# One core, attention-like pooling: the goods of a pair fetched in two transfers instead of four, and TensorE's wait for pooled banks moved to the head of a round

## The reference

```python
outer = jnp.einsum('bi,bnj->bnij', candidate_ad, goods).reshape(Bs, Ns, Ks * Ks)
k_b = jnp.broadcast_to(candidate_ad[:, None, :], (Bs, Ns, Ks))
h1 = jnp.concatenate((k_b, goods, outer), axis=-1)
act = jax.nn.sigmoid(h1 @ W1 + b1)
weight = act @ W2 + b2
out = jnp.sum(goods * weight, axis=1)
```

## Time and profile before

| what | value |
|---|---|
| median of 3 runs | 263.01 us (262.24 to 263.12) |
| the profiled execution's own time | 262.6 us |
| its span | 260.8 us |
| time around the span | 1.8 us |
| instructions | 18353 |

### The profile page before, as it was taken

One profiled execution on the slowest core, in us unless ns is written; L12 is line 12 of the kernel. 1 busy time (PEld: TensorE's weight loads), 2 busy tenths in 40 slices (PEclk: granted clock), 3 DMA queues, 4 the chain that ended last, 5 costly groups with the idle time before them and its releaser, 6 DMA issues.

```text
span 260.8 us, 18353 instructions
## 1 busy us (share of the span) xinstructions
PE 248.3 (95%) x7492; PEld 133.6 (51%) x7492; DVE 209.6 (80%) x1176; ACT 224.3 (86%) x658; POOL 147.0 (56%) x285
## 2 busy tenths in 40 slices
PE   6997989999999999999999999999999999999970
PEld 2335545455555555555555555555555555555540
DVE  0892568679888889888888888898888898888896
ACT  2898978978999999999999999999999999999940
POOL 1300664646766566665666666656666566665562
PEclk9999999999999999999999999999999999999996
DMA  5991876767778787777778887877777877887100
GB/s 209 284 322 29 248 221 181 224 189 232 242 225 239 224 225 237 234 238 227 223 221 244 227 249 207 239 232 240 229 233 224 230 237 233 238 230 224 53 1 10
DMA packets 38243, 55.10 MB, mean 211 GB/s; under 512 B 4256, under 2 KB 37920, under 8 KB 38048
## 3 DMA queue, kind: packets, MB, share of 16 engines
q1 hardware_dynamic: 37920, 54.41, 70.5%
q10 hardware_dynamic: 288, 0.32, 0.3%
HBM read 54.45 MB, written 0.26 MB: 210 GB/s over the span
## 4 chain that ended last, share of the span: by engine, by line
PE 87%; ACT 7%; DVE 2%; DMA 2%; issue 1%; ACTq 0%; DVEq 0%
PE w_ps L394 28%; PE z_ps L349 25%; PE x_ps L370 16%; PE w_ps L430 6%; PE x_ps L430 6%; PE s_ps L349 4%; ACT wm L485 4%; DMA act<-w_outer 2%; DVE goods L557 2%; ACT act L506 2%; ACT wxd L485 1%; PE z_ps L300 0%; ACT actx L514 0%; DVE whole L550 0%; PE z_ps L430 0%
## 5 line engine op out<-in xcount | busy, mean ns | idle before, releaser
L506 ACT ACTIVATE act<-z_ps,bias 128x200 f32<-128x200 f32 x384 | 129.4, 440 | 20.5 <-PE z_ps L349 10.9
L349 PE MATMUL z_ps<-goods,wm_ring 32*32 32x200 f32 x3072 | 80.3, 340 | 2.6 <-issue 1.2
L268 POOL TENSOR_TENSOR rest<-whole,top 128x200 f32<-128x200 f32 x64 | 36.3, 567 | 59.5 <-DVE top L552 35.9
L557 DVE CUSTOM_DVE_ANT_0 goods<-w_ps,goods 128x200 f32<-128x200 f32 x122 | 39.8, 364 | 30.8 <-PE z_ps L430 16.0
L394 PE MATMUL w_ps<-act,consts 128*32 128x200 f32 x1024 | 56.6, 339 | 0.7 <-ACT actx L514 0.7
L370 PE MATMUL x_ps<-goods,wx 128*32 128x200 f32 x1024 | 55.4, 333 | 0.0
L270 POOL TENSOR_SCALAR mid<-rest,consts 128x200 bf16<-128x200 f32 x64 | 50.3, 785 | 6.3
L349 PEld LDWEIGHTS z_ps<-goods,wm_ring 32*32 32x32 f32 x3072 | 30.3, 103 | 34.4 <-issue 33.0
L557 DVE CUSTOM_DVE_ANT_0 goods<-z_ps,goods 128x200 f32<-128x200 f32 x140 | 44.9, 361 | 0.0
L506 ACT ACTIVATE act<-s_ps,bias 128x200 f32<-128x200 f32 x128 | 44.9, 461 | 0.0
L246 POOL COPY wx<-wxd 32x96 f32<-32x96 f32 (+1 forms) x88 | 22.8, 259 | 37.0 <-PE x_ps L370 22.8
(11 more groups left out here) (45 smaller groups left out, 233.1 us busy)
## 6 DMA issues: line engine op xcount, KB each, us to landing
goods<-goods_t SPq DMA_DIRECT2D x256, 200.0 KB, 2.8
act<-cand_r SPq DMA_DIRECT2D x1, 1024.0 KB, 5.4
act<-cand_u SPq DMA_DIRECT2D x1, 256.0 KB, 3.0
candb<-cand_b SPq DMA_DIRECT2D x1, 256.0 KB, 3.8
out_t<-out_stage SPq DMA_DIRECT2D x4, 64.0 KB, 3.1
consts<-small ACTq DMA_DIRECT2D x1, 164.5 KB, 5.4
act<-w_outer ACTq DMA_DIRECT2D x1, 144.0 KB, 5.6
pick_sb<-pick SPq DMA_DIRECT2D x1, 128.0 KB, 3.5
```

The source lines that it names most:

```text
L268: nc.gpsimd.tensor_tensor(rest[:, :], whole[:, q % 2, :], top[:, q % 2, :], ALU.subtract).then_inc(part_step, 1)
L349: last = nc.tensor.matmul(z_bank(slot, r)[32 * c:32 * c + 32, N * s:N * s + N], wm_ring[32 * r:32 * r + 32, slot % RING, 4 * s + c, :], go ...
L506: last = nc.scalar.activation(act[:, p % A_SLOTS, r, N * s:N * s + N], z_bank(p, r)[:, N * s:N * s + N], ACT.Sigmoid, bias=bias[:, r, p, s ...
L557: one = nc.vector.tensor_tensor_reduce(goods[:, q % G_SLOTS, v, :], s_banks(q, f)[s][:, N * i:N * i + N], goods[:, q % G_SLOTS, v, :], 1.0 ...
```

## The change

Three things are edited:
1. The goods of a pair come in two transfers of four units (128 rows of 3200 bytes). Transfer j carries the four units of spread half f = j. For that the units of a pair are stored in the order of `place(v)`, 4f + 2s + i, in memory and in the tile; the host lays the input out so. `POOLED_ORDER` is gone.
2. Transfer j waits for both signals `pooled[j][0]` and `pooled[j][1]` and for one event three pairs back: `z_done` (the first bank of that pair) for j = 0, `z2_read` for j = 1. The signal of a full slot falls from 64 to 32.
3. In `products` the wait for `pooled[0][1]` and `pooled[1][1]` moves from the middle of round s = 0 to its head, and the second `pick_loaded` is gone.

```diff
+        def place(v):
+            s, f, i = v // 4, v % 4 // 2, v % 2
+            return 4 * f + 2 * s + i
...
                 if j == 0:
-                    sp.wait_ge(actx_done, i)
+                    sp.wait_ge(z_done, 4 * i + 1)
                 if j == 1:
-                    sp.wait_ge(z_done, 4 * i + 1)
-                if j == 2:
-                    sp.wait_ge(z_done, 4 * i + 4)
-                if j == 3:
                     sp.wait_ge(z2_read, i + 1)
             for p in range(PAIRS):
-                for j, v in enumerate(POOLED_ORDER):
+                for j in range(2):
                     if p >= G_SLOTS:
-                        f, s = divmod(j, 2)
-                        sp.wait_ge(pooled[f][s], POOLED_FROM[f][s] + p - G_SLOTS + 1)
+                        for s in range(2):
+                            sp.wait_ge(pooled[j][s], POOLED_FROM[j][s] + p - G_SLOTS + 1)
                     if p > AHEAD:
                         in_iteration(p - AHEAD, j)
-                    first = N * (PAIR_U * p + v)
-                    sp.dma_start(goods[:, p % G_SLOTS, v:v + 2, :].rearrange("p u n -> p (u n)"),
-                                 goods_t[:, first:first + 2 * N]).then_inc(goods_loaded[p % G_SLOTS], 16)
+                    first = N * (PAIR_U * p + 4 * j)
+                    sp.dma_start(goods[:, p % G_SLOTS, 4 * j:4 * j + 4, :].rearrange("p u n -> p (u n)"),
+                                 goods_t[:, first:first + 4 * N]).then_inc(goods_loaded[p % G_SLOTS], 16)
...
                         pe.wait_ge(z_read, p)
-                for r in range(4):
-                    if s == 0 and r == 2 and slot >= LAG + 1:
-                        pe.wait_ge(pick_loaded, 16)
+                    if slot >= LAG + 1:
                         pe.wait_ge(pooled[0][1], p)
                         pe.wait_ge(pooled[1][1], p)
+                for r in range(4):
                     for c in range(4):
                         last = nc.tensor.matmul(z_bank(slot, r)[32 * c:32 * c + 32, N * s:N * s + N],
                                                 wm_ring[32 * r:32 * r + 32, slot % RING, 4 * s + c, :],
-                                                goods[32 * r:32 * r + 32, slot % G_SLOTS, 4 * s + c, :],
+                                                goods[32 * r:32 * r + 32, slot % G_SLOTS, place(4 * s + c), :],
                                                 start=True, stop=True)
```

More of the change, by code:

```diff
@@ L32 @@
 RUN = 16
-POOLED_ORDER = (0, 4, 2, 6)
 C_W1G = 0
@@ L370, in products_x @@
                         last = nc.tensor.matmul(x_ps[32 * c:32 * c + 32, 0:N], left,
-                                                goods[:, slot % G_SLOTS, 4 * s + c, :], start=s == 0, stop=s == 1)
+                                                goods[:, slot % G_SLOTS, place(4 * s + c), :], start=s == 0, stop=s == 1)
                 last.then_inc(x_done, 1)
@@ L434, in _ @@
             for p in range(FILL):
-                products(p, p, 0, 64)
+                products(p, p, 0, 32)
                 if p >= LAG:
@@ L448, in _ @@
             pe.reg_mov(pair, FILL - 1)
-            pe.reg_mov(loaded, 64)
+            pe.reg_mov(loaded, 32)
             with pe.Fori(0, TURNS):
@@ L454, in _ @@
                     if slot == RING - 1:
-                        pe.reg_add(loaded, loaded, 64)
+                        pe.reg_add(loaded, loaded, 32)
                     p = pe.snap(pair, min_val=FILL, max_val=PAIRS - 1)
-                    products(p, slot + 1, 0, pe.snap(loaded, min_val=64, max_val=64 * (TURNS + 1)))
+                    products(p, slot + 1, 0, pe.snap(loaded, min_val=32, max_val=32 * (TURNS + 1)))
                     spread(p, slot + 1, 0)
@@ L557, in pool_unit @@
                 one = nc.vector.tensor_tensor_reduce(
-                    goods[:, q % G_SLOTS, v, :], s_banks(q, f)[s][:, N * i:N * i + N], goods[:, q % G_SLOTS, v, :],
+                    goods[:, q % G_SLOTS, place(v), :], s_banks(q, f)[s][:, N * i:N * i + N], goods[:, q % G_SLOTS, place(v), :],
                     1.0, 0.0, ALU.mult, ALU.add, out_stage[:, u:u + 1])
@@ L597 @@
     w1_cand, w1_goods, w1_out = w1[:K], w1[K:2 * K], w1[2 * K:].reshape(K, K, H)
-    goods = np.asarray(r_goods).reshape(UNITS, 4, N, K)
+    goods = np.asarray(r_goods).reshape(PAIRS, 2, 2, 2, 4, N, K).transpose(0, 2, 1, 3, 4, 5, 6).reshape(UNITS, 4, N, K)
     goods_t = np.ascontiguousarray(goods.transpose(1, 3, 0, 2)).reshape(P, UNITS * N)
```

## The result

Faster, but by about half of what was forecast: 260.64 us (median of 16 runs, 259.83 to 261.88) against 262.95 (16 runs of the kernel before beside it, 261.35 to 264.05), 2.3 us less. The ratio is 0.9931, with a 95% interval of 0.9913 to 0.9948. The ratio is an estimate of its own, not the quotient of the two medians (that would be 0.9912); by the ratio the change is worth 1.8 us, and by its interval 1.4 to 2.3. The forecast was 258.8, 4.2 us less. The profiled execution of the change took 260.44 us, with a span of 258.7.

The account below looks back on a forecast made before the run. TensorE was taken as the bound, busy in every microsecond of the steady stretch. 263.0 - 4.2 for the shorter rounds, with head waits and transfers at 0, gave 258.8 us; own range 257.8 to 259.8, wide range 257.6 to 261.2.

Parts of the forecast that it names:

- wide range of 257.6 to 261.2: Range for the whole time, taking in the forecast's own range and rival B with some scatter, leaving out C, D and E.
- rival B: At every head TensorE reacts more slowly to the pooled signal: each 0.03 us late, 1.8 in all, 260.6 us; chance 0.10.
- 60 x 0.07 = 4.2 us less: Waits leave the middle of round s = 0 in 60 pairs from 4 on, saving 0.07 us each; ends 3.6 and 4.8.
- the control with pair 3: Pair 3's round s = 0 has no wait in its middle and takes 0.57 us, implying a gain of 0.06 a pair.
- I cost it at 0 us: Waits moved to the head of round s = 0: pooled signal allows a start 0.06 us before the array is free.
- The transfers at 0: SP's 128 merged goods transfers in place of 256 cost 0 us: 6.96 us left, landing in 2.8 to 5.6 median.
- C: The shorter round in `products` isn't kept, through another engine or the head's place: 263.0 us, chance 0.08.
- D: The head becomes bound by DVE, 0.14 us late, 0.07 net a pair, + 4.2 us: 267.2 us, chance 0.07.
- E: In the loop's first turn, fewer, larger transfers free the DMA engines; up to 3.0 us come back: 255.8 us, chance 0.03.
- The rule on splitting: Splitting transfers starts some sooner with mostly idle DMA engines; merging delays goods, the sum unchanged while delay is under 6.96 us.
- The sentence of the Trainium skill on a taken branch: A sequencer fetches code by DMA in blocks and a taken branch can stall; such stops are gone after the first turn.

Follow-up runs that it names:

- e4: The change itself, measured again without any edit, for a second profile: 260.32 us, ratio 0.9924 to the kernel before.
- e5: The change, but in the first pair of every loop turn the pooled waits stay in the middle of the round: 260.39 us, ratio 0.9943.
- e12: The kernel before with the pooled waits at the head, except in each loop turn's first pair; still four transfers: 259.81 us, ratio 0.9897.
- e1: The kernel before with only the pooled waits moved to the head, goods still in four transfers: 259.61 us, ratio 0.9888.
- e11: The change plus one 160-column memset on DVE ahead of the last two units of every pair: 264.21 us, ratio 1.0072.
- e8: The change plus three one-column memsets on DVE ahead of the last two units of every pair: 259.92 us, ratio 0.9920.
- e13: The kernel before with only the pooled waits moved to the head, measured again on another chip: 259.10 us, ratio 0.9873.
- e3: The change, but the goods of pairs 0 to 5 still come in transfers of two units: 259.30 us, ratio 0.9897.
- e16: The change with transfers of two units for pairs 0 to 5, measured again on another chip: 260.05 us, ratio 0.9889.

## Why the prediction failed

The direction was right and the size was not: 2.3 us in place of 4.2 by the medians, 1.8 by the ratio. 260.64 lies outside the forecast's own range of 257.8 to 259.8, and over the 259.8 from which the prediction called itself wrong. It lies inside the wide range of 257.6 to 261.2 only because that range took in rival B, whose 260.6 it hits by luck: B's mechanism did not occur. Point by point:

- **"60 x 0.07 = 4.2 us less."** The size of one pair was nearly right: the round fell from 0.63 to 0.57, the period from 3.57 to 3.50. The waits alone give 0.062 of it, what the control with pair 3 said; that the sum's 0.07 was met as well is the merged transfers' 0.005, which the prediction had at nothing. The factor of 60 is not shown. The saving is seen in 52 pairs, from 11 to 63: 52 x 0.068 = 3.5. In the loop's first turn TensorE stands still for some 3 us anyway, and three profiles of the change give 38.4 to 38.5 from pair 1 to 11, against 38.3 and 39.1 before: between 0.7 less and 0.3 more, where 0.5 less was booked.
- **"I cost it at 0 us"**, the waits at the head. This is the step that failed most clearly. The reasoning about DVE's signal held: 0.17 between signal and head, reaction 0.11 to 0.12, 0.05 spare. But I looked at a head in the middle of a loop turn and took it for all. In the first pair of most turns TensorE's load comes 0.12 later although DVE's signal is on time, 182.93 - 52 x 3.504 = 0.7 us in the profile of the change, 0.9 in e4. That takes 0.7 to 0.9 of the 1.9 us by which 260.64 and 258.8 differ. In the kernel before the same hold-up, if it is there, lies beside work that TensorE already had in hand, because its last wait at the head is done 0.57 us ahead of the load. e5 and e12 show that the place of the wait decides whether the heads are late; what the hold-up is stays open.
- **The transfers at 0.** Their times at SP and their landing (3.4 us, inside 2.8 to 5.6) were right and no wait names them. Two pairs of runs on one chip still put the change 0.7 and 1.0 us above the waits alone. That part of the gap was not in the sum. It isn't clear of noise, and its mechanism isn't shown.
- **The sum by the runs:** 3.5 - 0.8 = 2.7 in the steady stretch; waits alone measured 3.0 and 3.8 under the kernel before beside them (262.59 - 259.61, 262.92 - 259.10), the change 2.3 to 2.8. The waits alone would have fallen inside the forecast's range. Of the rivals, B is out as written: it had all heads late by 0.03, and five in six are not late at all, while the sixth is late by 0.12. C and D are out, with a period of 3.50. E is out too; in three profiles of the change nothing came back from the first turn. In the two profiles compared, the steady stretch gives 2.9 us of gain, and 0.8 of it is lost again ahead of pair 11 (0.6 up to pair 1, 0.2 from there on), where profiles of one program differ by as much or more.
- **The rule on splitting** of the Trainium skill (Perfetto Trace Analysis, section DMA Optimizations) changed nothing in the steady stretch, as said: the merged transfers land some 6.96 - 3.4 = 3.5 us ahead of their need, the longest there (4.4) 2.5. The sentence of the Trainium skill on a taken branch (Runtime: NRT & Kernel Launch, section Instruction fetch mechanics) was read for the first turn alone. The late heads stand 1.7 us behind the loop's branch in later turns; whether that is a stall of the kind it describes, no view here can show.

## What to carry to other kernels

Moving a wait on the bounding engine from the middle of a burst to its head saved 0.062 us a time here. It also took away the 0.57 us by which the last head wait had been done ahead of the load, and a delay of 0.12 at the first head of most loop turns became visible. Before costing a moved wait at nothing, look at every distinct place it lands in, above all the first one of a loop turn, and not only at a typical one. And do not book a per-iteration saving for iterations in which the engine stands still for another reason. A profile is one execution: compare its own time with the median of the run before a stretch of it is taken for the program's.

## What the runs showed of the hardware

- A group of waits in the middle of 16 matmuls that would run side by side cost 0.062 us, though its signals were there (median distance of two heads, 3.572 to 3.510 in e1).
- TensorE's first weight load comes 0.11 to 0.12 us after the end of the DVE instruction whose signal it waits for (e11, median 0.115), and 0.12 after one of ACT.
- Three one-column memsets between two large DVE instructions put the next signal only some 0.03 us later (median 0.168 to 0.141 ahead of the head, e8), though each is listed with 0.06 us; one of 160 columns, listed with 0.19, put it 0.14 later (e11).
- The same bytes in rows of 3200 instead of 1600 bytes took the DMA engines less time: a share of 0.71 at 230 GB/s in the steady stretch, against 0.77 at 226. Twice the size landed in 3.4 us instead of 2.8. No engine waited for a transfer in the steady stretch, and the transfers alone left the time the same (1.0007 and 1.0020).
- The same program's time from pair 1 to pair 11 can repeat to 0.15 us (the change, the transfers alone) or differ by 0.8 to 1.8 us (the kernel before, e1 and e13, e3 and e16).
- In the first pair of a loop turn TensorE's load can come 0.25 us after its wait instruction for DVE, where 0.13 is usual (six of eight turns in the change). With 0.57 us between them it was never late (e5, e12 and the kernel before).
